# Attention's opening: the third unit's stack is loaded behind group 3's parts, and the feed-forward weights at step 100

## The reference, cut to what matters

```python
def attention(x):                                # x after a layer norm, (4, 1024, 256)
    k_eff = (W_dq.T @ W_uq.T @ W_uk).reshape(16, 16, 128)
    v_eff = transpose((W_uv.T @ W_o.T).reshape(128, 16, 16), (1, 0, 2))
    c_kv = x @ W_dkv.T
    q = (x @ W_dq.T @ W_uq.T).reshape(B, T, 16, 16)
    q_lat = einsum('bqhd,hdl->bhql', q, k_eff)
    attn = softmax(causal(einsum('bhql,bkl->bhqk', q_lat, c_kv) / sqrt(16)))
    y_lat = einsum('bhqk,bkl->bhql', attn, c_kv)
    return einsum('bhql,hld->bqhd', y_lat, v_eff).reshape(B, T, 256)
```

## Time and profile before

| | |
|---|---|
| median of 3 runs | 1328.22 us (1326.58 to 1328.77) |
| the profiled execution | 1327.01 us |
| its span, first to last instruction | 1324.9 us |
| mean granted TensorE clock | 0.959 of full speed |
| PE busy | 1187.6 us, 90% of the span |
| DVE busy | 842.5 us, 64% |
| ACT busy | 668.3 us, 50% |
| POOL busy | 386.5 us, 29% |

### The profile page before, as it was taken

How to read it: one execution, slowest core, us unless ns; L and a number is a source line. 1 busy time by engine, 2 the same in 40 slices (tenths; PEclk the granted TensorE clock), 3 DMA queues, 4 the chain that set the end, 5 groups by cost and what they waited for, 6 DMA issues and landing times. The chain is left out here.

```text
span 1324.9 us, 32379 instructions
## 1 busy us (share of the span) xinstructions
PE 1187.6 (90%) x13506; PEld 742.3 (56%) x13506; DVE 842.5 (64%) x1815; ACT 668.3 (50%) x1449; POOL 386.5 (29%) x614
## 2 busy tenths in 40 slices
PE   6769999999999999998899986867889878899995
PEld 3334444444444444433688874435666666788884
DVE  6666767676787787771554357696858473465346
ACT  4336666666666666666522245654554222352223
POOL 5421415141300000002352113644354421743210
PEclk9889999999999999998899997898999899999998
DMA  6882435454544444300000000102121201000003
GB/s 204 161 189 43 86 36 96 49 97 50 97 50 49 49 50 49 50 2 1 1 0 1 0 25 11 31 11 50 20 51 20 52 25 21 4 0 1 0 4 123
DMA packets 78753, 61.65 MB, mean 47 GB/s; under 512 B 41360, under 2 KB 65552, under 8 KB 78480
## 3 DMA queue, kind: packets, MB, share of 16 engines
q1 hardware_dynamic: 77456, 57.18, 24.3%
q10 hardware_dynamic: 1152, 2.41, 0.5%
HBM read 38.20 MB, written 20.97 MB: 45 GB/s over the span
## 5 line engine op out<-in xcount | busy, mean ns | idle before, releaser
L727 ACT ACTIVATE weights<-psum 128x512 f32<-128x512 f32 (+1 forms) x608 | 322.6, 584 | 162.0 <-PE psum L628 160.0
L777 DVE TENSOR_REDUCE maxima<-psum 128x1 f32<-128x512 f32 (+3 forms) x432 | 262.3, 662 | 52.6 <-PE psum L550 51.5
L628 PE MATMUL psum<-q_stack,k_stack 99*128 99x512 bf16 (+3 forms) x768 | 224.1, 329 | 0.8 <-ACT weights L727 0.7
L550 PE MATMUL psum<-k_stack,q_stack 96*128 96x512 bf16 (+3 forms) x768 | 213.3, 329 | 2.0 <-DVE maxima L777 2.0
L645 PE MATMUL psum<-weights,v_rows 128*17 128x512 f32 (+3 forms) x1536 | 162.5, 495 | 0.1
L522 POOL TENSOR_TENSOR residual<-residual,att_o 128x256 f32<-128x256 f32 x32 | 23.2, 725 | 357.6 <-DVE att_o L810 357.6
L1011 PE MATMUL psum<-f_xT,f_weights_hi 128*128 128x512 f32 x384 | 122.9, 402 | 4.4 <-DVE f_weights_lo L955 2.3
L1053 ACT ACTIVATE f_gates<-psum,ffn_biases 128x512 f32<-128x512 f32 x72 | 49.5, 689 | 141.0 <-PE psum L1017 133.4
L777 DVE TENSOR_REDUCE negmax<-psum 128x1 f32<-128x384 f32 (+3 forms) x176 | 102.3, 635 | 28.3 <-PE psum L550 26.6
L628 PEld LDWEIGHTS psum<-q_stack,k_stack 99*128 99x128 bf16 x768 | 72.5, 98 | 83.3 <-ACT weights L727 37.9
L1093 DVE TENSOR_TENSOR f_state<-f_gates 128x512 f32<-128x512 f32 x32 | 27.2, 849 | 139.8 <-POOL f_gates L970 90.4
(11 more groups left out here) (164 smaller groups left out, 2209.2 us busy)
## 6 DMA issues: line engine op xcount, KB each, us to landing
qk_parts<-a_parts SPq DMA_DIRECT2D x32, 384.0 KB, 4.3
q_stack<-qk_parts SPq DMA_DIRECT2D x90, 128.0 KB, 7.3
k_stack<-qk_parts SPq DMA_DIRECT2D x90, 128.0 KB, 8.0
residual<-in_x SPq DMA_DIRECT2D x8, 512.0 KB, 7.5
out_x<-residual SPq DMA_DIRECT2D x8, 512.0 KB, 2.9
ffn_weights<-in_ffn_w ACTq DMA_DIRECT2D x1, 2048.0 KB, 8.7
systems<-d_attnT_k_kb_v SPq DMA_DIRECT2D x32, 64.0 KB, 1.9
d_systems<-systems SPq DMA_DIRECT2D x4, 512.0 KB, 3.4
```

Source lines behind the costliest of these rows:

```text
L550: m = e.matmul(out[:, i * width:(i + 1) * width], self.qst[st][0:self.ROWS, h, qb * P:(qb + 1) * P], self.kst[st][0:self.ROWS, h, k0:k0 + ...
L628: m = e.matmul(out[:, j * width:(j + 1) * width], self.kst[st][0:self.ROWS + self.MAX_ROWS, h, kb * P:(kb + 1) * P], self.qst[st][0:self.R ...
L727: e.activation(self.weights[n % 2][:, heads[0]:heads[-1] + 1, 0:width], bank[self.score_bank[n, i]][:, 0:len(heads) * width].rearrange("p ...
L777: e.tensor_reduce(to, bank[self.bank[item]][:, 0:len(heads) * width].rearrange("p (h x) -> p h x", h=len(heads)), AXIS_X, ALU.max, negate= ...
```

## The change

In the prologue, SP loads the stack of unit 1 behind the last parts of group 1, as before, but that of unit 2 only behind the last parts of group 3. ACT issues the three loads of the feed-forward weights at the start of step 100 of attention instead of at the end of the prologue. No instruction is added or removed.

```diff
-    EARLY = 4
+    EARLY, FFN_LOAD = 4, 100
...
-            if item == ("qk", 1, *self.PROJECTED[-1]):
-                for u in range(1, STACKS):
+            for u, g in ((1, 1), (2, 3)):
+                if item == ("qk", g, *self.PROJECTED[-1]):
                     load(u, (0, 1))
...
         for item in self.prologue:
             copy_out(item)
-        k.load_ffn_scalar(e)
         for n, items in enumerate(self.during):
+            if n == self.FFN_LOAD:
+                k.load_ffn_scalar(e)
             for mine, i in self.mixed(n):
```

## The result

The changed kernel takes 1317.59 us in the median of four runs (1316.44 to 1321.47) against 1328.49 us before. The ratio is 0.9923, with a 95% interval of 0.9902 to 0.9943: 10.2 us faster (7.6 to 13.0), where 9.6 was forecast. The profiled execution took 1316.44 us, with a span of 1314.3 us.

A forecast was written before the change was run, and what follows sets the result against it. PE bounds the kernel; in the opening it waits on part 8, queued behind unit 2's stack. Gains of 8.87 and 0.90 us less 0.2 took the median from 1328.22 to 1318.6 us, range 1316.0 to 1322.5.

The forecast's parts named there:

- Point 1: Prologue queue: part 8 issued at about 56.3, landing at 67.9; ACT's 9.92 us wait goes, 8.87 us gained.
- Point 2: Prologue, behind ACT's hi of part 12: DVE and PE follow; PE turns negmax at 75.31 instead of 84.18.
- Point 3: Opening, 70 to 90 us: PE's clock stays full, part 14's product gets 0.90 us shorter, shift 9.77 us.
- second rival: PE's clock falls between 75 and 83 us, losing 2.2 to 4.3 us; median 1321.7 us, chance 0.14.
- Point 4: End of the prologue: chain links keep their lengths, so first scores start at 82.68 instead of 92.45.
- Point 5: Unit 2's stack, moved later, lands at 100 to 107, wanted at 108.89 in step 9; no cost taken.
- The rival's price: Step 9: unit 2's stack lands so late that PE stands; 1333 us for a landing at 124, chance 0.05.
- Point 6: Step 100: ACT's three issues of feed-forward weights cost 0 to 1.33 us, taken as 0.2.
- The sum: Whole kernel: 9.77 us gained less 0.2 lost, so 9.6 us off the median, 1318.6 us.
- last sign of being wrong: Prediction is wrong if the shift of 9.8 us at 100 us is not there at 600.
- third rival: Attention's end and later stages take up the shift, all but 2 us: 1326 us, chance 0.06.

The follow-up runs named there:

- e3: Changed kernel, but six of unit 2's twelve stack loads stay behind group 1's parts, ahead of part 8; 1319.38 us, ratio 0.9939 to the kernel before.
- e5: Kernel before, its order of loads untouched, with six buffers of parts instead of four for groups 0 to 3; 1327.37 us, ratio 1.0.
- e2: Kernel before with only the feed-forward weights moved to step 100, unit 2's stack loads staying behind group 1's parts; 1329.02 us, ratio 1.0005.
- e9: The changed kernel run again, unedited, in a second series; 1319.89 us, ratio 0.9925 to the kernel before.
- e1: Kernel before with only unit 2's stack moved behind group 3's parts, weights still loaded at the end of the prologue; 1320.22 us, ratio 0.9943.
- e4: Changed kernel with unit 2's stack loaded too late on purpose, after step 7's exponentials; 1330.94 us, ratio 1.0018 to the kernel before.
- e10: Changed kernel with six buffers of parts instead of four, in a second series; 1319.28 us, ratio 0.9917 to the kernel before.
- e6: Changed kernel with six buffers of parts instead of four, first series; 1316.04 us, ratio 0.9911 to the kernel before.

## Why the prediction was right, point by point

*Point 1, part 8.* Right. It was issued at 56.40 (forecast 56.3) and landed at 67.6 (67.9); ACT took it up at 72.06 (71.89). e3 shows the queue in proportion, e5 shows that it is the buffer that is waited for, and e2 that nothing of this happens without the move of the stack.

*Point 2, DVE and PE.* Right, and 0.4 us better than worked out, because not every link kept its length. The combination on DVE ended at 74.79 and not at 75.21. It took 0.18 us, and the 0.77 of the earlier trace rows was not its own length. In the kernel before, POOL was at the lo of part 12 when the combination started, and both ended together (84.05 and 84.08). In the changed kernel the combination was ahead of POOL's 74.72:

```profile
82.90 1.15 POOL L506 TENSOR_TENSOR a_parts<-a_rest,a_parts 128x512 bf16<-128x512 f32 x1 [13.99 <-ACT a_parts L671]
```

```profile
74.61 0.18 DVE L783 TENSOR_TENSOR negmax<-maxima 128x16 f32<-128x16 f32 x1
```

e3 has the same picture (0.75 us, ended at 77.76, POOL at 77.73). So this part of the gain, 0.59 us of DVE, was not in the reasoning.

*Point 3, the clock.* The product for part 14 took 1.02 us, as said. That the window 70:90 would be at full clock throughout was wrong for the profiled execution, where the clock fell for 3.4 us from 82.3 on, just when full work began. It cost 10.24 - 8.60 = 1.6 us, less than the 2.2 to 4.3 us of my second rival, but by the same mechanism. The stretches in which PE stood in the 8 us before the fall were 0.68, 0.52, 0.21 and 0.76 us. In e9, the same kernel with the same four, and in e1 it did not fall there. So it is neither certain nor excluded: the rival belongs to single executions and not to the kernel.

*Point 4, to the first scores.* Right: 82.21 against 82.68, released by the max DMA as before. The max DMAs went 10.24 us earlier. The wait ahead of the scores was 0.76 us, where I had said some 2.

*Point 5, unit 2's stack.* Right. It landed 11 us ahead of its use, at 99.1, just under the 100 to 107 that I gave. The rival's price is e4's: the whole wait, and 2.5 us of low clock on top, which I had left out.

*Point 6, the weights.* The 0.2 us that I took were nothing in ACT's timeline: it issued beside a running exponential. e2 (1.0005) and e1's opening show no effect of the second half of the change. The intervals leave room for 2 or 3 us.

*The sum.* 9.6 us were forecast, and the two series measured 0.77% and 0.75%, some 10 us. They agree, but part of the agreement is luck: in single executions the opening gave 8.60 and 9.84 us, and what follows attention moved this to 11.90 and 8.73. My last sign of being wrong, a shift that is gone at 600 us, did not come: it was 8.34 and 9.49 us at unit 15's max DMAs. My third rival, the gain given back later, is real in a small form. Between the two markers single profiles moved from 3.3 us ahead (the change) to 4.4 us back (e5). e2 shows it too, since its opening is nearly that of the kernel before and its shift still goes from 0.43 to 1.34 us.

The clock explains a part of this. From unit 15's max DMAs to SP's load of `d_conv` (768.44 in the kernel before), the low clock lasted 17.1 us in six of the twelve profiles and 13.6 us in the other six. The stretch took 175.6 to 176.1 us in the former and 174.0 to 174.8 in the latter. Behind it the picture is less clean: the changed kernel's profile gained 3.8 us in the delta-rule layer, and profiles with nearly as little low clock there (e1, e2, e10) gained 0.1 to 1.1. So the cause of this gain is open.

## What to carry to other kernels

When several engines wait in a ring behind one late buffer, look at the queue that its transfer stands in, and at what stands ahead of it without being needed yet: moving that cost nothing here, and with the loads moved two more buffers brought nothing that could be measured. A wait that is only moved to just ahead of dense TensorE work may win nothing, because the low clock that follows it then falls on the work (e5: 6.37 us won, 3.52 us left). For effects of under 3 us, compare markers in the traces at the end of the changed stage, and not only medians.

## What the runs showed of the hardware

- Loads of 128 KB, all on one queue, each put off what stood behind them by 1.1 us, with the DMA share at 1.1. For loads of 64 KB, issuing half of them from another engine did not bring them in earlier (landing 4.9 to 5.1 us after the issue instead of 2.9 to 3.0).
- DMA issues of ACT overlapped with its running instruction: the issue at 377.79 stood beside the exponential of 377.78 to 378.38, and the three issues of step 100 cost nothing in ACT's own timeline.
- PE's clock fell at 82 us in one execution of the changed kernel and not in another, with the same waits ahead of it, none over 0.76 us. It was the same with e6 and e10 at 66 us, there behind a wait of 1.77 us.
- A stall of 9.90 us in dense work cost 12.4 us, with 2.5 us of it by the low clock behind the stall (e4 against e9).
- DVE's combination L782, of 128x16 numbers in SBUF, took 0.17 to 0.18 us alone. Where POOL's lo (L506) was already running it took 0.48 to 0.77 us and ended 0.03 to 0.04 us behind it. In the kernel before this was so at 83.31, 264.91 and 337.29 us, and at none of the other thirteen.
